# Attention scores and a mixture of experts in one kernel: batch 0's second normalisation moved ahead of batch 1's top-k work on all engines

## The reference

```
n1  = layernorm(x)                                   # its rows are the "adjacency"
Q,K = ctx @ Wq.T, ctx @ Wk.T                         # ctx is 256 x 64, 4 heads of 16
sim = sum over heads of Q K^T, scaled                # 256 x 256
thr = the 76th largest value of each row of sim      # top 30%
A   = sigmoid(sim) * (sim >= thr);  A = (A + A^T)/2
x1  = x + (1-g)*n1 + g*A                             # g = sigmoid(gamma)
z   = layernorm(x1)
s   = softmax(z @ gate.T)                            # 8 experts, the best 2 count
out = x1 + sum over the 2 experts of s_e * W2_e(silu(W1_e z) * (W3_e z)) + the same of a shared expert
```

## Time and profile before

| what | value |
|---|---|
| runs | 116.21, 116.22, 116.55 us, median 116.22 |
| profiled execution | 115.1 us, span from first to last instruction 113.3 us |
| TensorE (PE) busy | 104.7 us, 92% |
| VectorE (DVE) busy | 85.7 us, 76% |
| GpSimd (POOL) busy | 70.4 us, 62% |
| ScalarE (ACT) busy | 62.5 us, 55% |
| mean granted TensorE clock | 0.970 |

### The profile page before, as it was taken

How to read it: one execution, slowest core, us unless ns; L and a number is a source line. 1 busy time by engine, 2 the same in 40 slices (tenths; PEclk the granted TensorE clock), 3 DMA queues, 4 the chain that set the end, 5 groups by cost and what they waited for, 6 DMA issues and landing times.

```text
span 113.3 us, 2526 instructions
## 1 busy us (share of the span) xinstructions
PE 104.7 (92%) x824; PEld 102.2 (90%) x824; DVE 85.7 (76%) x278; ACT 62.5 (55%) x157; POOL 70.4 (62%) x141
## 2 busy tenths in 40 slices
PE   6999618989999998999999999999999999999990
PEld 6799608978999998999999999999999999999990
DVE  6689779799998799967829999739536989456631
ACT  4179999989769864459793218233512452035400
POOL 4047688795964996599898494596109442283700
PEclk9999975599999999999999999999999999999999
DMA  1699993000002800000009100010281103830002
GB/s 35 157 343 365 363 362 108 3 6 3 0 0 72 292 14 0 3 0 6 0 4 301 68 3 6 26 66 0 64 299 50 64 3 95 270 103 0 0 0 93
DMA packets 8158, 10.33 MB, mean 91 GB/s; under 512 B 1936, under 2 KB 6544, under 8 KB 8144
## 3 DMA queue, kind: packets, MB, share of 16 engines
q1 hardware_dynamic: 7776, 10.13, 27.7%
q10 hardware_dynamic: 368, 0.04, 0.3%
HBM read 9.09 MB, written 1.08 MB: 90 GB/s over the span
## 4 chain that ended last, share of the span: by engine, by line
PE 75%; ACT 12%; DVE 8%; issue 2%; POOL 0%; POOLq 0%
PE ps_h L1378 22%; PE ps_u L1378 21%; PE ps_y L1406 20%; PE ps_a L1406 3%; PE ps_c L1345 3%; PE ps_u L1269 2%; ACT qkT L578 2%; ACT up_hi L556 1%; ACT sig L605 1%; PE ps_a L1316 1%; PE ps_b L1328 1%; DVE near L968 1%; DVE chosen L1085 1%; PE ps_h L1278 1%; ACT sides L627 1%
## 5 line engine op out<-in xcount | busy, mean ns | idle before, releaser
L453 POOL TENSOR_TENSOR gc<-prod,weights 128x512 f32<-128x512 f32 x16 | 25.8, 1630 | 16.4 <-DMA weights<-gates 9.2
L703 ACT ACTIVATE sil<-ps_h 128x512 f32<-128x512 f32 (+1 forms) x20 | 10.9, 552 | 16.7 <-PE ps_h L1378 16.7
L714 ACT ACTIVATE g_hi<-gc 128x512 fp32r<-128x512 f32 x16 | 10.0, 627 | 16.4 <-POOL gc L453 16.4
L1406 PE MATMUL ps_y<-dn_hi,g_hi 128*128 128x256 f32 x63 | 17.8, 283 | 0.0
L1406 PE MATMUL ps_y<-dn_hi,g_lo 128*128 128x256 f32 x63 | 17.7, 281 | 0.0
L1406 PE MATMUL ps_y<-dn_lo,g_hi 128*128 128x256 f32 x63 | 17.7, 280 | 0.0
L1130 DVE TENSOR_TENSOR g_lo<-gc,g_hi 128x512 fp32r<-128x512 f32 x16 | 13.9, 866 | 3.1 <-ACT g_hi L714 2.5
L1378 PE MATMUL ps_h<-z_hi,up_hi 128*128 128x256 f32 x72 | 15.3, 294 | 0.4 <-DVE prod L1118 0.4
L1378 PE MATMUL ps_h<-z_lo,up_hi 128*128 128x256 f32 x72 | 14.5, 282 | 0.2 <-DVE z_lo L1061 0.2
L1378 PE MATMUL ps_u<-z_hi,up_hi 128*128 128x256 f32 x72 | 14.4, 281 | 0.0
L1378 PE MATMUL ps_u<-z_hi,up_lo 128*128 128x256 f32 x72 | 14.4, 281 | 0.0
(11 more groups left out here) (199 smaller groups left out, 252.8 us busy)
## 6 DMA issues: line engine op xcount, KB each, us to landing
weights<-gates SPq DMA_DIRECT2D x8, 512.0 KB, 4.8
x_sb<-in_x SPq DMA_DIRECT2D x4, 256.0 KB, 6.3
up_raw<-in_w1t SPq DMA_DIRECT2D x4, 256.0 KB, 5.7
up_raw<-in_w3t SPq DMA_DIRECT2D x4, 256.0 KB, 5.9
dn_raw<-in_w2t SPq DMA_DIRECT2D x4, 256.0 KB, 6.3
out_x<-fin SPq DMA_DIRECT2D x3, 256.0 KB, 2.1
out_x<-fin SPq DMA_DIRECT2D x2, 128.0 KB, 1.7
ctx_sb<-in_ctxT SPq DMA_DIRECT2D x1, 192.0 KB, 4.7
```

What stands on the lines that cost most here:

```text
L453: nc.gpsimd.tensor_tensor(gc[k % 2][:, :].rearrange("p (n t q) -> p n t q", n=2, t=T), prod[s][:, :].rearrange("p (n t q) -> p n t q", n=2 ...
L703: nc.scalar.activation(sil[i % 2][:, :w], ps_h[i % 2][:, :w], ACT.Silu).then_inc(silu_ready, 1)
L714: nc.scalar.activation(g_hi[s][:, :], src[:, :], ACT.Copy).then_inc(ghi0_ready if s == 0 else ghi_ready, 1)
L1406: last = nc.tensor.matmul(dst[:, t * D:(t + 1) * D], g[s][:, tok], w[:, e, :], start=(s == 0 and first and m == 0), stop=(s == SLOTS - 1 a ...
```

## The change

On four engines the calls for batch 0's z are put ahead of calls for batch 1 or for later weights, and TensorE's `sum_hits(1)` is put behind `up(0, 0)`, with one `keep_warm(1)` taken out. No instruction but that one is added or dropped.

```diff
@@ GpSimd
             norm1(1)
+            norm2(0)
             lower_gate()
-            norm2(0)
             make_routing_consts()
             find_hits(1)
             lower_up(0, 1)
@@ ScalarE
             copy_scores(2)
+            high_z(0)
             upper_down(1)
             upper_up(3, 0)
-            high_z(0)
             copy_scores(3)
@@ VectorE
             lower_up(1, 1)
+            norm2_first()
             count_above(1)
-            norm2_first()
             drop_above(1)
             take_near(1, 0)
+            low_z(0)
             take_near(1, 1)
             read_hits(1)
-            low_z(0)
             select(1)
@@ TensorE
             similar(3)
             keep_warm(7)
-            sum_hits(1)
-            keep_warm(1)
             transpose_z(0)
             keep_warm(4)
             up(0, 0)
+            sum_hits(1)
             logits(0)
             keep_warm(1)
             transpose_masked(1)
```

## The result

| | before | after |
|---|---|---|
| median | 116.22 us | 118.42 us (117.70 to 118.70) |
| profiled execution, its span | 115.1, 113.3 us | 117.7, 115.9 us |
| mean granted TensorE clock | 0.970 | 0.971 in that execution, 0.956 in the three others |

The ratio is 1.0214, with a 95% interval from 1.0165 to 1.0263: the changed kernel is 2.2 us slower, outside the predicted range.

What follows compares the result with a forecast made beforehand. TensorE, fully busy from 43 us, was taken as the bound. Late by 0.67 less a vanished wait of 0.60 gives +0.07: 115.2 us for the profiled execution, 116.3 as median (1.1 above), range 115.3 to 117.7.

Steps and rivals of the forecast that it cites:

- Parts 1 to 4: Batch 0's z to batch 1's mask, all engines: up(0, 0) over 1.04 us earlier, the mask 1.13 us late.
- The 1.13 us of delay: VectorE, batch 1's mask: masked at 27.88 instead of 26.75, bounds 0.41 and 1.59 us.
- Part 5: TensorE behind batch 1's mask: 0.67 us late at batch 1's z, less an old wait of 0.60: +0.07 us.
- D: Rival, slower: idleness ahead of the masked transposes drops TensorE's clock to 1.2 GHz, 118.7 us; chance 0.07.
- Part 3: TensorE and ScalarE, batch 0's transposes at once: z_lo begins at 24.7, up(0, 0) over at 26.35, 1.04 us earlier.
- B: Rival, slower: GpSimd's gc starts ahead of VectorE's chosen, up(1, 0) late by 1.13 us, 117.35 us; chance 0.35.
- case A: The forecast: chosen gets through ahead of gc, old wait vanishes, 116.3 us, own range 115.8 to 116.7; chance 0.43.
- Rival C: Faster: the hits delay the mask by only 0.41 us, 0.65 gained, 115.55 us; chance 0.15.
- The bound: TensorE busy without a gap from 43 to 103 us; ahead of it its queue decides, and VectorE has no gap.

Runs made afterwards that it cites:

- with the sum ahead: Changed kernel with sum_hits(1) put back ahead of up(0, 0), behind keep_warm(4): median 116.57 us, runs of two kinds.
- the gate's wait: Changed kernel with GpSimd's gate(0, 1) also waiting for VectorE's prod of slot 3 of batch 0: 117.02 us, ratio 1.0138.
- The filled gap: Changed kernel with keep_warm(5) instead of keep_warm(1) ahead of transpose_masked(1): 116.04 us, ratio 1.0011 to the kernel before.
- all mends: Changed kernel with sum_hits(1) ahead of up(0, 0), keep_warm(5) ahead of transpose_masked(1), and gate(0, 1) behind prod of slot 3: 115.72 us, ratio 1.0003.

## Why the prediction was wrong

The forecast was 116.3 us, no change that can be told; it came out 118.42.

- **Parts 1 to 4 were right.** z at 21.69 (said 21.78), `z_lo` 24.64 (24.7), the end of `up(0, 0)` 26.30 (26.35), the hits read at 26.96 (27.0), the mask at 27.86 (27.88). The 1.13 us of delay, the term on which all hung, measured 1.11. Taken away one at a time, the place of the sum is worth 0.30 and the register load 0.25; these need not add up, because with the sum ahead `kth_pick`, held beside GpSimd's `up_lo`, sets the mask as much as the load does. The rest goes with z's and `z_lo`'s turns ahead of the search and was not taken apart further.
- **The step that failed is in Part 5**: "TensorE idles nearly 1 us ahead of it", priced at nothing but the lateness of the masked transposes. The clock fell in that idle time. It measured half clock from 28.20 to 31.60 us, and 1.17 us of TensorE's time behind the 0.37 of lateness. This stood among the rivals as D with a chance of 0.07 and "the stretch around is busy" against it; that was the wrong argument, for two more idle times of the weight loads lay in front of it (0.34 and 0.88 us, ahead of `up(0, 0)` and of its `z_lo` matmuls), the second made by the change's own earlier start, and it follows from the starts in Part 3. The first of them isn't needed: in the profile with the gate's wait the clock fell without it. The second seems to be: with the sum ahead, where it is gone, the clock held over 1.07 us at the mask in the profiled execution, though not, by their mean clocks, in all. The profiled execution shows the fall, and the mean clock of the three others, 0.956, speaks for it. D's price for the clock itself, 2.5 us, was too high: 1.17 here, 1.5 with the gate's wait. That D's 118.7 us comes near the measured 118.42 is chance, since the measured time has the second held instruction in it.
- **B and D were taken for separate cases.** Their prices were added to nothing. In truth the fallen clock decides the race: with TensorE 1.5 us late instead of 0.67 `route_a(1)` no longer meets the start of the first gc but both, 0.95 us more. The clock and the later mask, with the port relieved, gave 117.0.
- **The rest of Part 5 was right once the clock is held.** The filled gap gives 42.95 for `up(1, 0)`, 42.82 less the execution's own lateness, where case A has 43.03, and the kernel's time is then the same as before (1.0011).
- **Rival C fell**: it needed a delay of the mask under 0.7 us, and that measured 1.11; and even with all mends the microsecond that `up(0, 0)` gains never reaches the end.
- **The bound was named half.** I said that VectorE has no gap and that TensorE's queue decides. Both are true, but the change speeds up batch 0's way to TensorE at the expense of batch 1's way through VectorE, and that way had only 0.46 us to spare.

## What to carry to other kernels

Before an item is moved ahead on all engines, ask which item it is moved past and how much that one has to spare at the place where it is next waited for; here it was 0.46 us, and the move cost it 1.1. Price an idle time of the matmul engine twice: once for what starts late, and once for the clock, the idle times just before it included; cheap matmuls that compute nothing took the ratio from 1.0214 back to 1.0011. A value read into a register needs work queued on that engine between the read and its use, and a reordering that takes this work away pays for it though no instruction is added.

## What was not expected of the hardware

- A fall of the clock can hang on a quarter of a microsecond: in the changed kernel with an idle time of 0.93 us (weight loads) ahead of the masked transposes the kernel took 117.7 to 118.7 us, without the register load, with 0.67 there in the profiled execution, it took 115.4 to 116.2 or 117.4 to 118.2. What came before counts too: with 1.07 us at the same place and no idle time just ahead the clock held in the profiled execution. The median of such a kernel says little.
- Instructions of 16 elements that take 0.17 us took 1.28 and 1.04 us under a gc on GpSimd that reads SBUF. The Trainium skill, "SBUF — State Buffer", Summary: rules for kernel authors, has it that of a VectorE instruction with two SBUF inputs and a GpSimd one that reads SBUF the second to issue fully blocks until the first finishes; the rows agree, the held ones ended within 0.1 us of the end of their gc (43.04 for `lgd`, the second gc having started at 42.97).
- The kernel before itself takes between 114.6 and 116.8 us with nothing changed, and the tail of these kernels, where the gates of the last batch go through DRAM, has an idle time of TensorE of 0.6 to 0.9 us in some executions and none in others, with the trip through DRAM 0.3 to 0.5 us longer in the first. Local gains of 0.6 us ahead of it could not be told from none.
